# Folding the products of a deformable convolution in another layout, with its vertical distances computed one chunk earlier

## The reference

```python
om = conv3x3(x, w_off) + b_off                 # 27 channels: 9 dy, 9 dx, 9 masks
py, px = off_y + h + ky, off_x + w + kx        # where each of the 9 taps samples
sampled = bilinear(x, py, px) * sigmoid(mask)  # 0 outside the image
out = einsum("bckhw,ock->bohw", sampled, w)    # then + b, batch norm, relu, + x
```

## Time and profile before

| what | value |
|---|---|
| median of 3 runs | 832.03 us (831.27 to 839.7) |
| the profiled execution | 829.57 us, span 827.4 us |
| PE, DVE, ACT, POOL busy | 620.5, 624.9, 530.4, 560.5 us |
| first fold of the 128 steps starts | 324.0 us |
| last second fold starts | 793.2 us |

### The profile page before, as it was taken

How to read it: one execution, slowest core, us unless ns; L and a number is a source line. 1 busy time by engine, 2 the same in 40 slices (tenths; PEclk the granted TensorE clock), 3 DMA queues, 4 the chain that set the end, 5 groups by cost and what they waited for, 6 DMA issues and landing times. The chain is left out here.

```text
span 827.4 us, 31946 instructions
## 1 busy us (share of the span) xinstructions
PE 620.5 (75%) x13480; PEld 474.7 (57%) x13480; DVE 624.9 (76%) x815; ACT 530.4 (64%) x838; POOL 560.5 (68%) x441
## 2 busy tenths in 40 slices
PE   5968888888699996776766767676876688577622
PEld 1325655655336664766766756675766677576622
DVE  3469999998522126788787889888888988889845
ACT  2646777776212326778688687887878788676705
POOL 3037888883230003789898999989889997988840
PEclk9988999999799999899999999989999989978867
DMA  4000000000085119668778667666765756657202
GB/s 170 1 0 2 1 0 0 0 0 0 18 209 119 20 19 213 147 141 195 176 165 197 155 164 186 160 160 163 174 174 156 183 157 153 168 145 187 77 4 101
DMA packets 40587, 92.29 MB, mean 112 GB/s; under 512 B 21263, under 2 KB 21391, under 8 KB 40208
## 3 DMA queue, kind: packets, MB, share of 16 engines
q1 hardware_dynamic: 37314, 89.57, 43.7%
q10 hardware_dynamic: 3150, 0.88, 0.5%
HBM read 79.47 MB, written 3.28 MB: 100 GB/s over the span
## 5 line engine op out<-in xcount | busy, mean ns | idle before, releaser
L1256 PE MATMUL PS<-region 64*64 64x112 f32 (+5 forms) x11136 | 378.1, 270 | 143.6 <-ACT region L1100 87.2
L1256 PEld LDWEIGHTS PS<-region 64*64 64x64 f32 (+1 forms) x11136 | 314.6, 144 | 202.5 <-ACT region L1100 112.7
L842 DVE TENSOR_TENSOR region<-PS,region 128x1024 f32<-128x1024 f32 (+1 forms) x256 | 299.2, 1204 | 66.0 <-PE PS L1256 60.2
L557 POOL TENSOR_TENSOR region<-region 128x960 f32<-128x960 f32 x128 | 239.6, 1872 | 54.8 <-DVE region L842 54.6
L1097 ACT ACTIVATE region<-region,cst 128x1152 f32<-128x1152 f32 x128 | 159.3, 1244 | 6.0 <-DMA region<-px_scratch 5.4
L1100 ACT ACTIVATE region<-region 128x1152 f32<-128x1152 f32 x128 | 149.1, 1164 | 9.2 <-PE PS L1256 3.3
L560 POOL TENSOR_TENSOR region<-region 128x320 f32<-128x320 f32 x128 | 117.0, 914 | 10.0
L853 DVE TENSOR_REDUCE region<-region 128x32 f32<-128x736 f32 x128 | 116.3, 909 | 1.3 <-POOL region L560 1.3
L1256 PE MATMUL PS<-wg,xp 64*64 64x144 f32 x1024 | 83.7, 295 | 1.1 <-issue 1.1
L486 POOL TENSOR_TENSOR region<-region,cst 128x1024 f32<-128x1024 f32 x32 | 61.4, 1918 | 31.3 <-PE PS L1331 25.2
L709 DVE SCALAR_TENSOR_TENSOR region<-region,wr (+4 forms) x57 | 73.8, 1295 | 0.1
(11 more groups left out here) (139 smaller groups left out, 626.4 us busy)
## 6 DMA issues: line engine op xcount, KB each, us to landing
region<-px_scratch SPq DMA_DIRECT2D x256, 288.0 KB, 4.7
out<-region SPq DMA_DIRECT2D x4, 512.0 KB, 3.0
region<-xp SPq DMA_DIRECT2D x8, 140.2 KB, 3.0
region<-xp SPq DMA_DIRECT2D x8, 140.1 KB, 2.9
region<-xp SPq DMA_DIRECT2D x8, 140.0 KB, 2.9
cst<-in_consts SPq DMA_DIRECT2D x1, 1102.5 KB, 8.9
region<-xp SPq DMA_DIRECT2D x8, 132.0 KB, 2.9
region<-xp SPq DMA_DIRECT2D x8, 131.9 KB, 2.8
```

What stands on the lines that cost most here:

```text
L557: pool.tensor_tensor(two_rows[:, :, :, 0:NA - FOLD], two_rows[:, :, :, 0:NA - FOLD], two_rows[:, :, :, FOLD:NA], ALU.add).then_inc(half_re ...
L842: v.tensor_tensor(uu[:, 2 * u:2 * u + 2, :, lo:hi], PS[:, banks:banks + 2, 0:(hi - lo) * C].rearrange("p h (a o) -> p h o a", o=C), awf[:, ...
L1256: return nc.tensor.matmul(o, l, r, start=start, stop=stop)
```

## The change

Three things change together.

1. `uu` is laid term by term: the 16 outputs of a term lie side by side. A product reads PSUM and writes `uu` in one order, and repeats each vertical weight over 16 elements.
2. The folds are 31 and 16 terms: the first adds terms 32 to 62 onto 0 to 30 (992 elements in two runs of 496). The second adds terms 16 to 31 to terms 0 to 15 (512 elements) and writes the sums output by output into the place of terms 32 to 47, so neighbouring sums of a term are written 16 elements (64 bytes) apart. The sum on DVE then takes 16 terms, 512 elements in place of 736.
3. `difference` runs two chunks ahead in place of one.

```diff
-FOLD = HALVES[1] + 1
-KEEP = FOLD - 10
+FOLD = HALVES[1]
+KEEP = FOLD // 2
...
+        uu = cut2(UB * 2 * NA * C).rearrange("p (u a o) -> p u a o", u=2 * UB, o=C)
+        def folded(two_rows):
+            return two_rows[:, :, FOLD:FOLD + KEEP].rearrange("p u a o -> p u (a o)").rearrange("p u (o a) -> p u o a", o=C)
...
             difference(0, 0, c_("jrel"), ad_ready)
+            pool.wait_ge(py_out, done(1, 2))
+            difference(0, 1, c_("jrel"), ad_ready)
...
-                    if n % SPC == 0:
-                        difference(s // NCH, s % NCH, c_("jrel"), ad_ready)
+                    if n % SPC == 0 and s + 1 < PAIRS * NCH:
+                        difference((s + 1) // NCH, (s + 1) % NCH, c_("jrel"), ad_ready)
...
-                pool.tensor_tensor(two_rows[:, :, :, 0:NA - FOLD], two_rows[:, :, :, 0:NA - FOLD],
-                                   two_rows[:, :, :, FOLD:NA], ALU.add).then_inc(half_ready, 1)
+                pool.tensor_tensor(two_rows[:, :, 0:NA - FOLD], two_rows[:, :, 0:NA - FOLD],
+                                   two_rows[:, :, FOLD:NA], ALU.add).then_inc(half_ready, 1)
                 pool.wait_ge(half_ready, n + 1)
-                pool.tensor_tensor(two_rows[:, :, :, 0:FOLD - KEEP], two_rows[:, :, :, 0:FOLD - KEEP],
-                                   two_rows[:, :, :, KEEP:FOLD], ALU.add).then_inc(fold_ready, 1)
+                pool.tensor_tensor(folded(two_rows).rearrange("p u o a -> p u a o"), two_rows[:, :, 0:KEEP], two_rows[:, :, KEEP:FOLD], ALU.add).then_inc(fold_ready, 1)
...
-                    uu[:, 2 * u:2 * u + 2, :, lo:hi], PS[:, banks:banks + 2, 0:(hi - lo) * C].rearrange("p h (a o) -> p h o a", o=C),
-                    awf[:, bass.ds(line, 2), lo:hi].unsqueeze(2).to_broadcast([P, 2, C, hi - lo]),
+                    uu[:, 2 * u:2 * u + 2, lo:hi], PS[:, banks:banks + 2, 0:(hi - lo) * C].rearrange("p h (a o) -> p h a o", o=C),
+                    end(awf[:, bass.ds(line, 2), lo:hi], C),
...
-                v.tensor_reduce(totals(2 * (n % STEPS), n // STEPS), uu[:, b:b + 2, :, 0:KEEP], AX.X, ALU.add).then_inc(os_ready, 1)
+                v.tensor_reduce(totals(2 * (n % STEPS), n // STEPS), folded(uu[:, b:b + 2]), AX.X, ALU.add).then_inc(os_ready, 1)
```

More of the change, by code:

```diff
@@ L45 @@
 HALVES = (0, CH // C, NA)
-FOLD = HALVES[1] + 1
-KEEP = FOLD - 10
-APITCH = NA
+FOLD = HALVES[1]
+KEEP = FOLD // 2
 PEND = H * HLANE
@@ L208, in build @@
         wt = cut2(2 * 2 * KK * W).rearrange("p (u q k s) -> p u q k s", u=2, q=2, k=KK)
-        uu = cut2(UB * 2 * APITCH * C).rearrange("p (u o a) -> p u o a", u=2 * UB, o=C)
-        band_rows = uu[:, 2].rearrange("p o a -> p (o a)")[:, 0:KK * NR * C].rearrange("p (k a) -> p k a", k=KK)
-        ind = uu[:, 0:2].rearrange("p u o a -> p (u o a)")[:, 0:UNITS]
+        uu = cut2(UB * 2 * NA * C).rearrange("p (u a o) -> p u a o", u=2 * UB, o=C)
+        band_rows = uu[:, 2].rearrange("p a o -> p (a o)")[:, 0:KK * NR * C].rearrange("p (k a) -> p k a", k=KK)
+        ind = uu[:, 0:2].rearrange("p u a o -> p (u a o)")[:, 0:UNITS]
+        def folded(two_rows):
+            return two_rows[:, :, FOLD:FOLD + KEEP].rearrange("p u a o -> p u (a o)").rearrange("p u (o a) -> p u o a", o=C)
         def xs_of(g):
@@ L894, in interpolate @@
                     part = small[:, 16:48].rearrange("p (y o) -> p y o", y=2)
-                    v.tensor_reduce(part, uu[:, 0:2, :, 0:NA], AX.X, ALU.add).then_inc(part_ready, 1)
+                    v.tensor_reduce(part, uu[:, 0:2].rearrange("p u a o -> p u o a"), AX.X, ALU.add).then_inc(part_ready, 1)
                     dve.wait_ge(part_ready, n + 1)
```

## The result

The changed kernel takes 886.7 us (median of 4 runs, 883.2 to 888.1); the kernel before, beside it, took 835.7 us (median of 4). The ratio is 1.061, with a 95% interval of 1.053 to 1.068. The forecast was 884 us. The profiled execution took 883.2 us, its span is 881.0 us (before 827.4), and its mean granted clock is 0.924 (before 0.925).

What follows compares the result with a forecast made beforehand. Engines waiting in turn, with POOL nearly full, bound the kernel. POOL's steps grow from 470.1 to 521.7 us, 1 us is left for first waits, the last sum gives 0.2 back: 884 us, range 795 to 900.

Steps and rivals of the forecast that it cites:

- The ring opens: ACT, PE, DVE and POOL wait in turn each chunk; an earlier difference removes ACT's 82 us and nearly all POOL's 43 us.
- line (a): POOL's folds priced from L514 and L572 at 2.12 ns an element: 2288 and 1269 ns, +0.77 us a step; chance 0.52.
- Line (b): POOL's folds priced from today's two folds, 1.50 ns an element: 1920 and 1201 ns, no change, 832 us; chance 0.12.
- Line (c): POOL's folds priced from rows with one input repeated, 1.65 ns: 1.87 and 1.07 us, 807 us; faster-kernel chance 0.28.
- POOL sets the time: In the steps POOL is full, busy over 95%, at 3.58 us a fold pair: 521.7 us against 470.1.
- The sum and the products on DVE: DVE's sum falls from 909 ns to 0.68 us, products stay at 1.2 us; hidden while POOL is slower.
- The scattered write: POOL's second fold writing 64 bytes apart: taken as 0; rival at full price 0.27 us a step, 918 us, chance 0.08.
- The granted clock: PE's clock should stay at 1.00 for more of the time, as long idle stretches go; no chance of its own.
- The rivals of a faster kernel: POOL's folds no dearer an element than today's row or one with a repeated input: 807 or 772 us; chance 0.28.
- the turning point: Queue time of a POOL fold pair, 3.15 us, 0.34 over today's: below it the kernel gets faster, above it slower.
- the 3 us of remaining waits: In the faster cases' sums, all that was left of POOL's waits in the steps once the earlier difference removed the rest.
- (e): Price of POOL's scattered write in the second fold: 0.53 ns an element, up to +0.27 us on 512 elements.

Runs made afterwards that it cites:

- e1_ahead_only: Kernel before with only the differences issued two chunks ahead, layout and folds of 30 and 10 terms kept: 804.4 us against 831.0, ratio 0.964.
- e2_folds_only: Changed kernel with the differences one chunk ahead again, new layout and folds of 31 and 16 terms kept: 889.7 us against 831.0, ratio 1.067.
- e3_probes: Changed kernel plus 44 unused POOL additions after all work, varying runs, pitch and input distance; the first fold's form took 2.27 us, that of before 1.83 us.
- e5_shifted: Changed kernel with terms from 32 up stored one element further on, first fold at distance 513 instead of 512: 841.3 us against 833.7, ratio 1.010.

## Why the prediction was right

- **The ring opens.** Right. `away`'s wait of 82 us went, and with the old folds this is worth 27 us (`e1_ahead_only`). With the new folds it is worth next to nothing (`e2_folds_only`), as POOL is then full in either case.
- **The price of the folds, line (a).** Right in size: 2294 and 1289 ns for 2288 and 1269. In queue a pair took 3.63 us, not 3.58. The reason given for the choice, that the row it rests on has the same form, was not the reason, so that it led to the right price was luck: at distances of 513 and 257 the same reasoning would have given the same 2288 and 1269 ns, and `e3_probes` took 1.94 and 1.10 us. Form and length of the runs hardly count; both new distances, 512 and 256, are multiples of 4 elements, and those cost 2.1 ns an element. The prediction saw that L557 has its inputs "33 elements apart, an odd number", and this was the right row to be puzzled by, with the wrong property: 33 leaves 1 on division by 4. Line (b), with its 1.50 ns an element, was drawn through a cheap fold (distance 33) and a dear one (distance 23), and so was a price of neither. Line (c), 1.65 ns an element where one input is repeated, was not tested.
- **POOL sets the time.** Right: 98% busy, and from the first fold (322.90) to the end of the last (847.74) 524.8 us, for 522.7 with the 1 us allowed.
- **The sum and the products on DVE** went as said, 685 and 1224 ns, and did not matter.
- **The scattered write** was taken as nothing, with 0.27 us kept for the high end. It costs 0.02 us, which is all that the second fold had over its forecast.
- **The granted clock** was expected at 1.00 for more of the time. Wrong: it is 0.92 over the steps, as before (0.92 in the stretch from 324 to 794 us). The waits for the hats went, but PE stands 146 us for DVE's products in their place. This cost next to nothing, as POOL is 98% busy all the same: from 725 to 730 us, at 0.50, POOL is busy for 4.92 of 5 us.
- **The rivals of a faster kernel** came out too fast. They let all but 3 us of POOL's waits come back. Near the turning point the sign holds: the folds of `e5_shifted` take 3.27 us of queue a pair (521.93 to 525.20), just above the 3.15 where the sign was to turn, and the kernel is slower, by 8 us where this sum gives 15. Well below it, at the 2.81 us of the old folds, the sum gives 788 us and the chip 804. The step that fails there is the 3 us of remaining waits: POOL still waits 19 us inside the steps, behind a wait of PE for "issue" that already took 31.0 us in the kernel before and is in none of the rows read for the prediction. 788.3 us is reached only once the transfers are small.

The Trainium skill, page "GPSIMD Engine Reference", section "Performance versus the Vector engine", gives two-input work about 2.6 cycles an element, by the prediction's estimate 2.17 ns. The runs come near it at dear distances (2.09 ns) and not at cheap ones (1.77 ns). Its 50% for reads with a step over 8 bytes, in "Performance pitfalls for Q7 kernels", does not carry over to this write: 1.28 us scattered, 1.26 contiguous. The prediction set that 50% beside the upper end of (e), and this was wrong: half of 1.27 us would be 0.63 us, not 0.27.

The best kernel measured that does all the work is `e1_ahead_only`, 0.964 of the time before.

## What to carry to other kernels

Before a layout is changed, work out for each f32 addition on POOL how far apart its two inputs lie, modulo 16 bytes (what is left on division by 16): a remainder of 4 or 8 bytes is about 15% cheaper than 0 or 12, and one element of padding buys it. Price a removed wait by what the next engine can still take up, and test the halves of a change apart: here one half gained 27 us and the other lost 59. When a wait is released by nothing that the profile shows, look at what the DMA queues carry at that time, the instruction queue among them, and make one run with smaller transfers.

## What the runs showed of the hardware

- An addition of two f32 inputs on POOL has two prices, by the distance of the inputs modulo 16 bytes: 0 and 12 bytes about 2.09 ns an element (992 elements 2.27 us), 4 and 8 bytes about 1.77 (1.94 us). Whether the result goes in place or elsewhere, where the first input starts and how the runs are cut changes it by about 5% at most in these probes.
- Writing 512 results 64 bytes apart from each other costs POOL 0.02 us.
- PE waited 69.9 us in all for "issue" with the DMA engines 71% busy over the steps, and 0.4 us with them 10% busy. Each of the 59 waits ended 1.22 to 1.69 us after the end of a 16 KB packet of instructions. With smaller loads the granted clock over the same 441 us rose from 0.95 to 0.97.
